# Swapping two groups of work in every fourth iteration: TensorE's first convolution of the next sample ahead of the kernels' products K, ScalarE's rounding of z ahead of K's evictions

## The chip, the cores and the metric

The kernel runs on one core of a Trainium2 chip. The metric is the device time of one execution in microseconds; of the runs of a kernel the median is taken. TensorE (PE) multiplies matrices into PSUM, ScalarE (ACT) and VectorE (DVE) work on tiles element by element, GpSimd (POOL) does small work of that kind, and SyncE (SP) issues the transfers. Each engine executes its own list of instructions strictly in order, and waits on semaphores that the others raise. All times are microseconds.

## The reference

The input x is 64 samples of 64 channels by 1024 points, with one style vector of 128 numbers for each sample. Four blocks follow one another, each `x = x + f(x, style)`. In f there are four layers, each a convolution whose weights are scaled per sample by the style and then normalised:

```python
s = style @ mw.T + mb
weight = SCALE * w * s[:, None, :, None]
demod = lax.rsqrt(jnp.sum(weight * weight, axis=(2, 3)) + EPS)
weight = weight * demod[:, :, None, None]
# 'same':       conv 3 taps + bias
# 'upsample':   transposed conv, stride 2, + bias, then blur (1,3,3,1)
# 'same':       conv 3 taps + bias
# 'downsample': blur (1,3,3,1), then conv, stride 2, + bias
```

The reference computes in float32.

## The kernel before

**Layout.** A sample is held as 128 x 513: the odd points of its 64 channels on partitions 0 to 63, the even ones on 64 to 127. There is no step between layers 1, 2 and 3 that is not linear, so the kernel composes them: for each sample it builds one short filter out of the weights of layers 1 to 3 and the blurs, and applies it to z, the output of layer 0. Near the two ends of a sample the composed filter is not exact, and small separate work ("edges") corrects a few columns.

**Precision.** Products are made in float32r, whose operands are rounded. Each operand is therefore split in two: ScalarE writes the rounded value (`...h`) and VectorE the rest (`...l`), and TensorE makes three products, h by h, h by l and l by h.

**Iterations.** The index n runs over 256 steps, 64 samples in each of the four blocks (in groups of 8 samples the blocks are done as a whole, so block k is n = 64k to 64k+63). For sample n:
- `xhi(n)` (ScalarE, line 733) and `xlo(n)` (VectorE, line 1036) scale and split x. Both are made three samples ahead.
- `conv0(n)` (TensorE): layer 0, 6 matmuls of 512 columns, the first four from xhi, the last two from xlo, into a PSUM bank, of which there are two (n mod 2).
- `zhi(n)` (ScalarE, line 747) and `zlo(n)` (VectorE, line 1042) split z and free that bank.
- `convg(n)` (TensorE): the composed filter, 12 matmuls of 512 columns: 8 with the filter's rounded part gh and 4 with its rest gl.
- `xnew(n)` (VectorE, line 1051): adds the result to x in SBUF; SyncE stores it. In the last block ScalarE has added a bias before that, `xb(n)` (line 755), and xnew waits for it.

**Quads.** The composed filters are built for four samples at a time (q counts these quads). `v_products(q)` (V, 9 matmuls of 256 columns) combines layers 3 and 2; ScalarE and VectorE scale and split the result (`vfull`, `vhi`, `vlo`); `k_products(q)` (K, 15 matmuls of 256 columns) brings in layer 1. V and K use the same two PSUM banks. ScalarE evicts K in two parts of four instructions, `kev(q, 0)` and `kev(q, 1)` (line 787). VectorE applies the blurs to it (`fir_even`, `fir_odd`, lines 1084 to 1096). Then `ghi(q)` (ScalarE, lines 804 and 809) rounds the filter, in two halves, `glo(q)` (VectorE, line 1119) makes the rests, two halves, each waiting for its rounding, and SyncE copies all four to the other half of the partitions. `w3hi` (ScalarE) and `w3s`, `w3lo` (GpSimd, lines 1371, 1377, 1378) prepare the operand of V.

**What sets the order.** Nothing but the code: each engine has a loop over n that calls these functions in a written order. `g_at(n)` gives the quad whose K is made in iteration n: q = n/4 + 1 for n = 4, 8, ..., 248, that is always a quad's first iteration, and the filter is needed from iteration n+4 on. `v_at(n)` places V in iterations n = 4m+1. The first quad's work is spread over a prologue, with exceptions (`V_LATE`, `G_LATE`, `FIRST_GHI = 3`): the filters of quad 1 (samples 4 to 7) are rounded by ScalarE in iteration 3.

TensorE's order in iteration n = 4m is: K(m+1), conv0(n+1), any set-up or edge products, convg(n). ScalarE's order is: w3hi, xhi(n+3), kev part 0, (in iteration 3: ghi(1)), zhi(n+1), kev part 1, ghi, vfull, vhi, xb(n). VectorE's loop (not touched by the change) is: vlo, xlo(n+3), xnew(n-1), in iteration 4m+1 fir_even, then zlo(n+1), fir_odd with xlo behind it, glo. VectorE's prologue ends with xlo(4), vlo(2), glo(1), xlo(5), xnew(2), zlo(4), xlo(6).

Waits that matter here: zhi(n) waits for conv0(n) and for convg(n-2); conv0(n) waits for xhi(n), for zlo(n-2), and ahead of its last two matmuls for xlo(n); convg(n) waits for zlo(n), for xnew(n-2) and for the copies of its filter; V(q) waits for kev(q-1).

Of the kernel before, what the change touches and what calls it, by code (L numbers as in the profile page):

```python
# [27 lines left out]
NN = NS * GS  # L28
NQ = NN // QS
V_LEAD, G_LEAD = 7, 4  # L30
V_LATE, G_LATE = {2: 1}, {1: 0}
# [59 lines left out]
def build(nc, x, ends, pack, taps, w3in, small, sets, out):  # L91
    ctx = ExitStack()
    with ctx:
# [129 lines left out]
        def v_at(n):  # L223
            if n in V_LATE or n in V_LATE.values():
                return (V_LATE[n] + V_LEAD) // QS if n in V_LATE else None
            q, i = divmod(n + V_LEAD, QS)
            return q if i == 0 and 0 <= q < NQ else None

        def g_at(n):
            if n in G_LATE or n in G_LATE.values():  # L230
                return (G_LATE[n] + G_LEAD) // QS if n in G_LATE else None
            q, i = divmod(n + G_LEAD, QS)
            return q if i == 0 and 0 <= q < NQ else None
# [45 lines left out]
        def setup_at(n):  # L279
            k, i = n // NB + 1, n % NB  # L280
            if k == NBLK - 1 and i == LAST_BIAS_S:
                return k, (BIAS_S,)
            return (k, (SECOND_SLOTS if k == 1 else SETUP_SLOTS).get(i, ())) if k < NBLK else (None, ())
# [108 lines left out]
        def _(pe):  # L392
# [67 lines left out]
            def add(out_ap, a, b, first=False, last=False):  # L460

                return pe.matmul(out_ap, a, b, start=first, stop=last, skip_group_check=True)  # L462

            def conv0(n):

                conv0_high(n)
                conv0_low(n)

            def conv0_high(n):
                k, o = where(n)[1], ps[:, ZP + n % 2, :]  # L470
                ah, al, h = w0h[:, k % NW], w0l[:, k % NW], xh[n % 3]
                pe.wait_ge(s["xhi"], n + 1)
                if n >= 2:
                    pe.wait_ge(s["zlo"], n - 1)
                for d in range(2):
                    add(o, ah[:, 2 * d:2 * d + 2, :], h[:, d:d + M], first=(d == 0))
                if n % NB == 0:
                    pe.wait_ge(s["w0l"], k + 1)
                for d in range(2):
                    add(o, al[:, 2 * d:2 * d + 2, :], h[:, d:d + M])  # L480

            def conv0_low(n):
                k, o = where(n)[1], ps[:, ZP + n % 2, :]
                ah, l = w0h[:, k % NW], xl[n % 3]
                pe.wait_ge(s["xlo"], n + 1)
                for d in range(2):
                    m = add(o, ah[:, 2 * d:2 * d + 2, :], l[:, d:d + M], last=(d == 1))
                m.then_inc(s["conv0"], 1)
# [67 lines left out]
            def k_products(q):  # L556

                k = STEPS[q * QS // GS][1]
                h, l, d, dl = w1h[:, k % NW], w1l[:, k % NW], w1d[:, k % NW], w1dl[:, k % NW]
                k6, k45, k23, k01 = (ps[:, VG + i // 2, i % 2 * QS * C:(i % 2 + 1) * QS * C] for i in range(4))  # L560
                early, late = slice(0, 2), slice(2, 4)
                pairs = ((k01, early, 0), (k23, late, 0), (k23, early, 1), (k45, late, 1))
                pe.wait_ge(s["w1hi"], k + 1)
                pe.wait_ge(s["vf"], q + 1)
                pe.wait_ge(s["vh"], q + 1)
                for i, (at, w, o) in enumerate(pairs):
                    add(at, h[:, w, :], vh[:, o, :, :], first=i in (0, 3))
                pe.wait_ge(s["w1l"], k + 1)
                for at, w, o in pairs:
                    add(at, l[:, w, :], vh[:, o, :, :])  # L570
                pe.wait_ge(s["vlp"], q + 1)
                for at, w, o in pairs:
                    add(at, h[:, w, :], vl[:, o, :, :])
                pe.wait_ge(s["vl"], q + 1)
                add(k45, d[:, early, :], vh[:, 2, :, :])
                add(k45, dl[:, early, :], vh[:, 2, :, :])
                add(k6, d[:, late, :], vh[:, 2, :, :]).then_inc(s["K"], 1)
# [65 lines left out]
            idle_products(14)  # L643
            pe.wait_ge(s["z0"], 1)
            for n in range(NN):
                if g_at(n) is not None and n not in G_LATE:
                    k_products(g_at(n))
                if n == 0:
                    conv0_low(1)
                    convg(0)  # L650
                    k_products(1)
                elif n + 1 < NN:
                    conv0(n + 1)
                if n in V_LATE:
                    v_products(v_at(n))
                k, stages = setup_at(n)
                for stage in stages:
                    setup(k, stage)
                if n == FIRST_BIAS_U:
                    setup(0, BIAS_U)  # L660
                k, stage = edge_at(n)
                if k is not None and stage < 3:
                    edge(k, stage)
                    for job in behind(k, stage):
                        setup(*job)
                if n > 0:
                    convg(n)
                if k is not None and stage == 3:
                    edge(k, stage)
                    for job in behind(k, stage):  # L670
                        setup(*job)
                if v_at(n) is not None and n not in V_LATE:
                    v_products(v_at(n))
# [3 lines left out]
        def _(act):  # L677
# [45 lines left out]
            def xhi(n):  # L723
                st, k, b, sl = where(n)
                act.wait_ge(s["S0"], k + 1)
                if k == 0:
                    p, use = pair_of(n)
                    act.wait_ge(s_in[p], 16 * use)
                else:
                    act.wait_ge(s["eap"], applied(st))  # L730
                if n >= 3:
                    act.wait_ge(s["conv0"], n - 2)
                act.activation(xh[n % 3][:, 0:XW], X[:, sl, :], ACT.Copy, scale=tab["S0"][:, k, b:b + 1]) \  # L733
                    .then_inc(s["xhi"], 1)

            def zhi(n):
                st, k, b, sl = where(n)
                act.wait_ge(s["conv0"], n + 1)
                if k:
                    act.wait_ge(s["bv2"], k + 1)  # L740
                elif n >= FIRST:
                    act.wait_ge(s["rest"], 1)
                else:
                    act.wait_ge(s["bx0"], 1)
                if n >= 2:
                    act.wait_ge(s["convg"], n - 1)
                act.activation(zh[n % 2][:, ZPAD:ZPAD + M], ps[:, ZP + n % 2, :], IDENT,  # L747
                               bias=tab["bx"][:, k, b:b + 1]).then_inc(s["zhi"], 1)
# [140 lines left out]
            for n in range(2, NN):  # L889
                if v_at(n + 1) is not None and n + 1 not in V_LATE:  # L890
                    w3hi(v_at(n + 1))
                if n + 3 < NN:
                    xhi(n + 3)
                if g_at(n) is not None:
                    kev(g_at(n), 0)
                if n == FIRST_GHI:
                    ghi(g_at(n - 2))
                if n + 1 < NN:
                    zhi(n + 1)
                if n in V_LATE:  # L900
                    vfull(v_at(n))
                    vhi(v_at(n))
                if g_at(n) is not None:
                    kev(g_at(n), 1)
                if g_at(n - 2) is not None and n != FIRST_GHI:
                    ghi(g_at(n - 2))
                if v_at(n - 1) is not None and n - 1 not in V_LATE:
                    vfull(v_at(n - 1))
                    vhi(v_at(n - 1))
                k, stages = setup_at(n - 1)  # L910
                if RECIP in stages:
                    setup(k, RECIP)
                k, stages = setup_at(n)
                for stage in stages:
                    if stage != RECIP:
                        setup(k, stage)
                if n == FIRST_VAR:
                    act.wait_ge(s["Dp"], 1)
                    act.activation(var[:, :, FIRST:], fl[:, 512:512 + LC].rearrange("p (l b) -> p l b", b=NB)[:, :, FIRST:], IDENT,
                                   bias=eps[:, 0:1], scale=SCALE * SCALE).then_inc(s["var0"], 1)  # L920
                if n == FIRST_ROOT:
                    root(slice(0, NLAY), NPART, slice(FIRST, NB))
                if where(n)[1] == NBLK - 1:
                    xb(n)
# [734 lines left out]
```

## Time and profile before

| | us |
|---|---|
| median of 3 runs | 1302.7 |
| lowest and highest | 1302.08, 1303.91 |
| the profiled execution | 1303.89 |
| its span | 1302.0 |
| TensorE busy in the span | 1291.3 (99%) |
| VectorE busy | 1101.5 (85%) |
| ScalarE busy | 922.4 (71%) |
| GpSimd busy | 359.1 (28%) |

The span runs from the first to the last instruction of the program; the execution's time is 1.9 longer. The mean granted clock of TensorE is 0.998 of its full 2.4 GHz. A matmul's record begins when it starts and ends when its results are out; the next matmul starts before that, so the records of back-to-back matmuls overlap, and the distance from start to start is the pace.

### The profile page before, as it was taken

To read this page: it belongs to the slowest core of one execution; us is meant where nothing else is said; L and a number is where in the kernel's file an instruction comes from. 1 tells how busy PE (TensorE), PEld (TensorE's weight loads), DVE (VectorE), ACT (ScalarE), POOL (GpSimd) and SP (SyncE) were. 2 spreads that over 40 slices of the span, in tenths; PEclk is the share of its full clock that TensorE was granted. 3 is DMA by queue.
4 is the path that set the end of the run, shared out by engine and by line. 5 is a ranking of instruction groups with operands and counts; after the bars stand their busy time and mean duration, and the time that the engine had idled before them with its cause. 6 is when DMAs were issued, how large, how long until landed. Compare 5 with 4: busy or idle time off the path is not lost.

```text
span 1302.0 us, 20375 instructions
## 1 busy us (share of the span) xinstructions
PE 1291.3 (99%) x6553; PEld 1076.5 (83%) x6553; DVE 1101.5 (85%) x1795; ACT 922.4 (71%) x1773; POOL 359.1 (28%) x640
## 2 busy tenths in 40 slices
PE   8999999999999999999999999999999999999998
PEld 6888888888888888888888888888888888888887
DVE  7999888998898889878889798988878878888885
ACT  6767576676675766766767667667677787787784
POOL 5142311141313212115222222122422252322311
PEclk9999999999999999999999999999999999999999
DMA  9354465545564455655446554556554276565543
GB/s 327 103 168 119 144 179 165 164 116 164 174 174 144 123 155 166 182 151 168 130 152 177 153 164 121 154 172 174 161 158 128 77 159 188 163 189 156 165 126 96
DMA packets 95369, 203.39 MB, mean 156 GB/s; under 512 B 10720, under 2 KB 12256, under 8 KB 95264
## 3 DMA queue, kind: packets, MB, share of 16 engines
q1 hardware_dynamic: 95040, 201.91, 54.0%
q8 instruction: 54, 0.88, 0.3%
q14 instruction: 51, 0.42, 0.1%
q10 hardware_dynamic: 224, 0.18, 0.0%
HBM read 72.39 MB, written 67.24 MB: 107 GB/s over the span
## 4 chain that ended last, share of the span: by engine, by line
PE 98%; DVE 1%; ACT 0%; issue 0%; POOL 0%; POOLq 0%; DVEq 0%; ACTq 0%
PE ps L462 96%; PE ps L586 1%; PE ps L398 1%; DVE scr L945 0%; ACT gh L815 0%; ACT vf L771 0%; PE ps L420 0%; DVE scr L955 0%; DVE scr L954 0%; DVE xl L1036 0%; DVE w2l L1245 0%; DVE w3q L1163 0%; ACT xh L733 0%; POOL scr L1416 0%; POOL scr L1415 0%
## 5 line engine op out<-in xcount | busy, mean ns | idle before, releaser
L462 PE MATMUL ps<-zh,gh 128*128 128x512 f32 (+1 forms) x1028 | 407.0, 396 | 0.2 <-ACT gh L815 0.2
L462 PE MATMUL ps<-zl,gh 128*128 128x512 f32 (+1 forms) x1028 | 405.5, 394 | 0.0
L747 ACT ACTIVATE zh<-ps,t_bx 128x512 fp32r<-128x512 f32 x256 | 175.3, 685 | 285.4 <-PE ps L462 284.4
L462 PE MATMUL ps<-zh,gl 128*128 128x512 f32 (+1 forms) x1028 | 282.2, 395 | 0.0
L787 ACT ACTIVATE kp<-ps,t_T1s 64x256 f32<-64x256 f32 x508 | 210.6, 463 | 66.3 <-PE ps L462 61.4
L1051 DVE SCALAR_TENSOR_TENSOR X<-ps,t_D,X 128x512 f32<-128x512 f32 x255 | 190.1, 745 | 61.1 <-PE ps L462 34.6
L462 PEld LDWEIGHTS ps<-zh,gh 128*128 128x128 f32 x1028 | 193.9, 189 | 46.9 <-DVE zl L1042 1.3
L462 PEld LDWEIGHTS ps<-zl,gh 128*128 128x128 f32 x1028 | 194.1, 189 | 45.0
L462 PEld LDWEIGHTS ps<-zh,gl 128*128 128x128 f32 x1028 | 194.0, 189 | 45.1
L1042 DVE SCALAR_TENSOR_TENSOR zl<-ps,t_bx,zh 128x512 fp32r<-128x512 f32 x256 | 190.7, 745 | 42.9 <-ACT zh L747 40.2
L1377 POOL TENSOR_TENSOR w3h<-w3q,w3h 64x256 fp32r<-64x256 f32 x63 | 69.1, 1097 | 548.5 <-ACT w3h L761 535.0
L1036 DVE SCALAR_TENSOR_TENSOR xl<-X,t_S,xh 128x513 fp32r<-128x513 f32 x256 | 190.7, 764 | 2.5
L733 ACT ACTIVATE xh<-X,t_S 128x513 fp32r<-128x513 f32 x256 | 183.3, 716 | 1.2
L462 PE MATMUL ps<-xl,w0h 128*128 128x512 f32 x512 | 160.6, 395 | 2.8 <-DVE xl L1036 2.8
L462 PE MATMUL ps<-xh,w0l 128*128 128x512 f32 x512 | 161.1, 396 | 0.0
L462 PE MATMUL ps<-xh,w0h 128*128 128x512 f32 x512 | 161.1, 395 | 0.0
L1084 DVE SCALAR_TENSOR_TENSOR gf<-kp,gf 128x384 f32<-128x384 f32 x256 | 153.2, 598 | 6.7
L1119 DVE TENSOR_TENSOR gl<-gf,gh 64x896 fp32r<-64x896 f32 x126 | 137.9, 1094 | 16.9 <-ACT gh L809 14.4
L809 ACT ACTIVATE gh<-gf 64x896 fp32r<-64x896 f32 x126 | 120.0, 952 | 3.6
L462 PEld LDWEIGHTS ps<-xl,w0h 128*128 128x128 f32 x512 | 96.0, 188 | 26.6 <-issue 2.3
L462 PEld LDWEIGHTS ps<-xh,w0l 128*128 128x128 f32 x512 | 96.4, 188 | 23.3
L462 PEld LDWEIGHTS ps<-xh,w0h 128*128 128x128 f32 x512 | 87.4, 188 | 11.4
(226 smaller groups left out, 1494.5 us busy)
## 6 DMA issues: line engine op xcount, KB each, us to landing
out_x<-X SPq DMA_DIRECT2D x255, 256.5 KB, 5.2
X<-out_x SPq DMA_DIRECT2D x96, 513.0 KB, 7.1
gh<-gh SPq DMA_DIRECT2D x127, 240.0 KB, 3.0
gl<-gl SPq DMA_DIRECT2D x127, 240.0 KB, 3.7
X<-x_in SPq DMA_DIRECT2D x32, 513.0 KB, 7.2
pk<-taps_in SPq DMA_DIRECT2D x3, 512.0 KB, 12.3
pk<-pack_in SPq DMA_DIRECT2D x3, 352.0 KB, 12.5
pk<-sets_in SPq DMA_DIRECT2D x4, 256.0 KB, 8.4
```

The lines of the kernel that those rows point to most:

```text
L398: m = pe.matmul(fl[h * C:(h + 1) * C, at:at + n], a, b, start=first, stop=last, skip_group_check=True)
L462: return pe.matmul(out_ap, a, b, start=first, stop=last, skip_group_check=True)
L733: act.activation(xh[n % 3][:, 0:XW], X[:, sl, :], ACT.Copy, scale=tab["S0"][:, k, b:b + 1]) \
L747: act.activation(zh[n % 2][:, ZPAD:ZPAD + M], ps[:, ZP + n % 2, :], IDENT, bias=tab["bx"][:, k, b:b + 1]).then_inc(s["zhi"], 1)
L787: return act.activation(kp[rows, to, i, :], got[of, :, j, :], ACT.Copy, scale=tab["T1s"][of, k, b:b + 1])
L809: act.activation(dst, gf[rows], ACT.Copy).then_inc(s["gsh"], 1)
L1036: dve.scalar_tensor_tensor(xl[n % 3][:, 0:XW], X[:, sl, :], tab["S0"][:, k, b:b + 1], xh[n % 3][:, 0:XW].bitcast(F32), ALU.mult, ALU.subtr ...
L1042: dve.scalar_tensor_tensor(zl[n % 2][:, ZPAD:ZPAD + M], ps[:, ZP + n % 2, :], tab["bx"][:, k, b:b + 1], zh[n % 2][:, ZPAD:ZPAD + M].bitcas ...
L1051: dve.scalar_tensor_tensor(X[:, sl, 0:M], ps[:, OP + n % 2, :], tab["D3"][:, k, b:b + 1], X[:, sl, 0:M], ALU.mult, ALU.add).then_inc(s["xn ...
L1084: return dve.scalar_tensor_tensor(dve_out, kp[rows, of, i, :], factor, dve_out, ALU.mult, ALU.add)
L1119: dve.tensor_tensor(dst, gf[rows], own(gh, h)[1].bitcast(F32), ALU.subtract).then_inc(s["gsl"], 1)
L1377: link(pool.tensor_tensor(w3h[C:128, 1], w3q[C:128, 1], hi[C:128, 1], ALU.subtract))
```

## The change

In TensorE's loop the two lines that call `k_products` move behind the block that calls `conv0(n + 1)`. In ScalarE's loop the two lines that call `zhi(n + 1)` move ahead of those that call `kev(.., 0)` and, in iteration 3, `ghi`.

```diff
@@ TensorE's loop
             for n in range(NN):
-                if g_at(n) is not None and n not in G_LATE:
-                    k_products(g_at(n))
                 if n == 0:
                     conv0_low(1)
                     convg(0)
                     k_products(1)
                 elif n + 1 < NN:
                     conv0(n + 1)
+                if g_at(n) is not None and n not in G_LATE:
+                    k_products(g_at(n))
                 if n in V_LATE:
                     v_products(v_at(n))
@@ ScalarE's loop
                 if n + 3 < NN:
                     xhi(n + 3)
+                if n + 1 < NN:
+                    zhi(n + 1)
                 if g_at(n) is not None:
                     kev(g_at(n), 0)
                 if n == FIRST_GHI:
                     ghi(g_at(n - 2))
-                if n + 1 < NN:
-                    zhi(n + 1)
                 if n in V_LATE:
                     vfull(v_at(n))
```

## Rows read from the trace of the kernel before

**Rows 1.** The page, busy us (share of the span) x instructions of each engine
```profile
PE 1291.3 (99%) x6553; PEld 1076.5 (83%) x6553; DVE 1101.5 (85%) x1795; ACT 922.4 (71%) x1773; POOL 359.1 (28%) x640
```

**Rows 2.** Windows: stretch, its length, busy of each engine, PEclk, DMA share, GB/s
```profile
26.90:30.30 3.40, 3.40 (x10) 2.65 (x9) 3.27 (x7) 3.30 (x5) 1.28 (x1) 0.50 1.04 404
...
100.00:1200.00 1100.00, 1100.00 (x5607) 917.27 (x5606) 938.89 (x1522) 782.27 (x1504) 299.45 (x515) 1.00 0.55 155
```

**Rows 3.** Timeline of TensorE, first products of K: start, us, what, idle before
```profile
606.89 0.63 PE L462 MATMUL ps<-vh,w1h 128*128 128x256 f32 x4
...
626.50 0.63 PE L462 MATMUL ps<-vh,w1h 128*128 128x256 f32 x4
```

**Rows 4.** Timeline of TensorE, iterations 3 and 4
```profile
42.87 0.69 PE L462 MATMUL ps<-xl,w0h 128*128 128x512 f32 x2
...
46.18 0.64 PE L462 MATMUL ps<-vh,w1h 128*128 128x256 f32 x4
...
47.96 0.62 PE L462 MATMUL ps<-xh,w0h 128*128 128x512 f32 x2
...
48.89 0.63 PE L462 MATMUL ps<-xl,w0h 128*128 128x512 f32 x2
49.36 0.39 PE L462 MATMUL ps<-zh,gh 128*128 128x512 f32 x1
```

**Rows 5.** Timeline of ScalarE, an ordinary quad (n = 116): K's evictions
```profile
608.85 1.67 ACT L787 ACTIVATE kp<-ps,t_T1s 64x256 f32<-64x256 f32 x4 [0.69 <-PE ps L462]
...
611.25 1.67 ACT L787 ACTIVATE kp<-ps,t_T1s 64x256 f32<-64x256 f32 x4
```

**Rows 6.** Timeline of VectorE, the same quad: the first instruction of fir_even
```profile
613.73 0.73 DVE L1088 TENSOR_TENSOR kp<-kp 128x128 f32<-128x128 f32 x1
```

**Rows 7.** Timeline of VectorE, last block: xnew(192), zlo(195), zlo(239)
```profile
992.45 0.75 DVE L1051 SCALAR_TENSOR_TENSOR X<-ps,t_D,X 128x512 f32<-128x512 f32 x1 [1.77 <-ACT X L755]
...
1001.46 0.74 DVE L1042 SCALAR_TENSOR_TENSOR zl<-ps,t_bx,zh 128x512 fp32r<-128x512 f32 x1
...
1219.60 0.74 DVE L1042 SCALAR_TENSOR_TENSOR zl<-ps,t_bx,zh 128x512 fp32r<-128x512 f32 x1
```

**Rows 8.** Timeline of TensorE, last block: first products of convg(195), convg(239)
```profile
1002.38 0.39 PE L462 MATMUL ps<-zh,gh 128*128 128x512 f32 x1
...
1221.53 0.40 PE L462 MATMUL ps<-zh,gh 128*128 128x512 f32 x1
```

**Rows 9.** Timeline of ScalarE, iteration 3: ghi(1), zhi(4)
```profile
42.18 0.40 ACT L804 ACTIVATE gf<-kp 128x256 f32<-128x256 f32 x1
42.61 1.93 ACT L809 ACTIVATE gh<-gf 64x896 fp32r<-64x896 f32 x2
44.57 0.69 ACT L747 ACTIVATE zh<-ps,t_bx 128x512 fp32r<-128x512 f32 x1
```

**Rows 10.** Timeline of VectorE, end of its prologue: glo(1), xlo(5), zlo(4)
```profile
44.44 2.20 DVE L1119 TENSOR_TENSOR gl<-gf,gh 64x896 fp32r<-64x896 f32 x2
46.67 1.12 DVE L1036 SCALAR_TENSOR_TENSOR xl<-X,t_S,xh 128x513 fp32r<-128x513 f32 x1
...
48.37 0.74 DVE L1042 SCALAR_TENSOR_TENSOR zl<-ps,t_bx,zh 128x512 fp32r<-128x512 f32 x1
```

**Rows 11.** DMA issues: x count, KB each, median us to landing
```profile
gl<-gl SPq DMA_DIRECT2D x127, 240.0 KB, 3.7
```

**Rows 12.** Timeline of GpSimd, w3lo(3)
```profile
45.85 1.39 POOL L1377 TENSOR_TENSOR w3h<-w3q,w3h 64x256 fp32r<-64x256 f32 x1 [12.46 <-ACT w3h L761]
```

**Rows 13.** Timeline of TensorE, its two longest waits, and the pace after
```profile
18.38 0.73 PE L462 MATMUL ps<-xl,w0h 128*128 128x512 f32 x2 [0.67 <-DVE xl L1036]
...
25.36 0.70 PE L462 MATMUL ps<-xl,w0h 128*128 128x512 f32 x2 [2.09 <-DVE xl L1036]
...
27.20 0.63 PE L462 MATMUL ps<-zl,gh 128*128 128x512 f32 x1
27.62 0.63 PE L462 MATMUL ps<-zh,gh 128*128 128x512 f32 x1
```

## Prediction

> **What bounds the kernel now.** I read the page's busy times first, then the windows, then the timelines of single engines. TensorE is busy 99% of the span, VectorE 85%, ScalarE 71% [rows 1]. The windows say where the missing 1% lies: from 100 to 1200 us TensorE is busy for all 1100 us, at granted clock 1.00 [rows 2]; its idle time is at the two ends. A busy matmul record is longer than the distance to the next one, so short pauses could hide in it. The pace rules them out: K of one quad starts at 606.89, of the next at 626.50 [rows 3], 19.61 us, and of the 63 such distances more than 40 are 19.59 to 19.62; the longer ones hold set-up or edge products or lie at the start. So a quad is a fixed string of matmuls that never waits, and an order of the same matmuls cannot shorten it. What the change can do is add a wait, where a result that was just in time is asked for earlier or comes later. TensorE's lost time is never given back, since it has no later idle time to use up.
>
> **The change in an ordinary quad (n = 4m, from n = 8).** No instruction is added or removed and no DMA is touched; one group swaps places on each of two engines. Call the quad's start T (there K starts now). K lasts 1.78 us (46.18 to 47.96) and the convolution conv0 1.40 (47.96 to 49.36) [rows 4].
> TensorE: conv0(n+1) starts at T instead of T+1.78, K ends 1.40 later, convg(n) starts at T+3.18 either way. conv0(n+1) needs xhi, xlo of n+1 and zlo(n-1); the last is already waited for by convg(n-1), and VectorE makes xlo(n+1) back in iteration n-2, so that two whole iterations (1.40 of conv0 and 12 products of 0.235, 4.2 us each) lie between; 1.78 less of that does no harm. Cost 0.
> ScalarE: now the four evictions of kev part 0 run from T+1.96 (608.85) to 610.52, z fills the time to 611.25, and part 1 runs to 612.92, T+6.03 [rows 5]. After: z runs while TensorE is in K, at about T+1.5; the eight evictions start at K's end, 1.40 later, and run in one piece. The z between them (0.71 with its issue) is gone, so kev ends 1.40 - 0.71 = 0.69 later, T+6.72 or 613.61. What is queued behind it: xb in the last block, xhi(n+4), zhi(n+2); and VectorE's fir_even waits for kev. In blocks 0 to 2 fir_even starts at 613.73 now, behind xnew(n), which waits for convg(n) [rows 6]. 613.61 is still ahead of it: cost 0, by a margin of 0.12. If that cover were gone too, VectorE would be a little later, and it has 1 us or more in most quads before zlo(n+3) is asked for. V, the next user of the same PSUM banks, comes behind conv0(n+2) and two convg, at T + 3.18 + 2.82 + 1.40 + 2.82 = T+10.2, and kev's end at T+6.72 is far ahead. Cost 0.
>
> **The last block (n from 192).** Here xb(n) follows kev on ScalarE and VectorE's xnew(n) waits for xb (992.45, idle 1.77 before it, ended by xb [rows 7]). So there the 0.69 goes into VectorE's queue whole, up to zlo(n+3). For n = 192 that zlo ends at 1001.46 + 0.74 = 1002.20, and convg(195) starts at 1002.38 [rows 7, 8]: 0.18 to spare. 0.69 - 0.18 = 0.51, and 0.05 for the semaphore: a stall of **0.56 us**. The 14 other such pairs have 0.97 to 2.53 to spare; the usual one is 1219.60 + 0.74 against 1221.53, 1.19 [rows 7, 8]. None stalls. Bounds: 0 (something ahead of xnew gives the time back) to 0.69.
>
> **The start (n = 3 and 4).** This is the only place where a wait has no slack. In iteration 3 ScalarE makes ghi(1) and then z(4): 42.18, 42.61, 44.57 [rows 9]. After, z(4) stands ahead and must wait for conv0(4), whose last products are at 42.87 + 0.69 = 43.56 [rows 4]. z(4) then runs from 43.60 and ghi(1) from 43.60 + 0.59 = 44.19, 2.01 later than 42.18; its two roundings start at 44.62 and 45.60. VectorE's glo(1) (2.20 us for two) now starts at 44.44, when VectorE comes to it [rows 10]. It will have to wait for the first rounding: 45.61, which is 1.17 later. Behind it on VectorE stands xlo(5), at 46.67 now, for 1.12 us; after: 47.84 to 48.96.
> And conv0(5) is asked for 1.78 us earlier: it starts at 46.18, its first four products take 0.93, and its last two want xlo(5) at 47.11. They start at 48.96 + 0.09 = 49.05. Stall: 49.05 - 47.11 = **1.94 us**. Before, they started at 48.89 with xlo(5) ready at 47.79, so 1.10 of slack hid everything. K(2) and convg(4) follow, the latter at 51.3 instead of 49.36. zlo(4) (48.37 + 0.74 now [rows 10]) comes at 50.3, and gl(1), issued about 47.9 with 3.7 to landing [rows 11], at 51.6; its products are due at 53.2. No second wait.
> Bounds: xlo took 1.12 there and not 0.74 as zlo does. VectorE and GpSimd overlap at that place: GpSimd's w3lo runs 45.85 to 47.24 [rows 12]. With 0.74 in its place the stall is 1.56. Since w3lo waits for a rounding that stands behind ghi(1) on ScalarE, it moves along and I take 1.94. From above, a third rounding-long wait (0.95) gives 2.9; from below, 0 if the records hide a slack that I don't see.
> The Trainium skill (SBUF — State Buffer, "Who interferes with whom") says that a VectorE instruction with two SBUF inputs and a GpSimd instruction that reads SBUF exclude one another for their whole length. By it xlo(5), with X and xh from SBUF, is held as it is now; the 0.38 more in its row agrees.
>
> **Sum.** 1.94 + 0.56 = 2.5 us. The profiled execution took 1303.89 (span 1302.0 and 1.9 around it); after: 1306.4. The median of the runs is 1302.7, the profiled one at the upper end of 1302.08 to 1303.91, so against the median: **1305.2**. That is +0.19%, and I call no change what is within 0.2% (2.6 us), about what a measurement of this kernel can tell. The forecast lies just inside.
>
> **Rivals.**
> A, slower: the stall takes the clock down. TensorE's clock fell once inside the run: it idled 2.09 us before 25.36 [rows 13], and from 26.9 to 30.3 the clock was 0.50 [rows 2], its lower level of 1.2 GHz. Before 18.38 it idled 0.67 and the clock stayed up [rows 13]. My stall, about 1.8 of idle time, lies between, nearer to the 2.09. The price from the same place: 3.4 us of products at a distance of 0.42 to 0.43 (27.20 to 27.62 [rows 13]) are 8, and at the pace of 2.4 GHz (two in 0.47, 48.89 to 49.36 [rows 4]) each would take 0.234: 8 x 0.193 = 1.55 us. The place is n = 4; it decides from an idle time somewhere between 0.67 and 2.09. Time: 1302.7 + 4.0 = 1306.7. Against it: before 25.36 TensorE had also small products and another 0.24 of idle time behind it, here it is dense on both sides.
> The Trainium skill (TensorE: Matmul & The Clock Gate, "What's actually happening") ties the low level to a stretch in which TensorE was idle throughout. By that rule this stall would not be enough and the sum stays at 2.5; the trace's drop, behind a stall with work on both sides, speaks against reading it so strictly.
> B, no loss: xlo(5) comes in time, because glo(1) doesn't wait or because DMA-bound work at the start shifts. Then only the 0.56 of the last block is left, or 0: 1302.7 to 1303.3. For it: all of the 1.94 hangs on one instruction order. Against it: that order is fixed in the code, and each row of it is in the trace.
> C, faster: z made earlier removes waits of convg(n+1) for zlo(n+1). At two of 62 quads that zlo ends 0.05 us before it is used, elsewhere 0.3 or more, so TensorE's pauses for it total under 0.2 us. With neither stall: 1302.5; more only if the matmul pace itself (0.235 us per 512 columns) gets better, for which no row speaks.
> D, a stall in every quad of the last block: if VectorE lost the 0.69 and did not make it up by the next quad. 15 x (0.69 + what piles up) would be some 5 us, 1308. Against it: behind zlo(n+3) VectorE again waits for ScalarE's vhi, which is late by only some 0.3.
>
> **How the numbers follow.** Forecast 0.52, A 0.26, B 0.14, C 0.04, D 0.04. The forecast's own range is 1303.8 to 1306.3; its upper quarter (0.15) is over +2.6. Slower by over 0.2%: A, D and that quarter, 0.45. Faster by over 0.2%: 0.03. Within: 0.52. Range: 1302.6, which takes in most of B, to 1307.4, which takes in A with 0.7 for the spread of the runs.
>
> **What would show it.** In the trace after: TensorE idle about 1.8 us once, at 47.3, released by VectorE's xl line; the xl before it starts near 47.8, and ghi near 44.2. The granted clock around 50 us decides A. K to K stays 19.61 in ordinary quads. In the quad of n = 192 K to K is 0.5 longer. ScalarE's eight evictions in one piece of 3.35 us, ending 0.69 later within the quad. TensorE's work without waits (its start at 26.3 and its end at 1298) must be the same but for the two stalls. The prediction is wrong if xlo(5) is not what TensorE waits for at n = 4, if any ordinary quad is longer, or if the time is under 1302.5 or over 1307.5.

## The result and the profile after

The changed kernel takes 1306.43 us (median of 8 runs, 1305.16 to 1307.92), the kernel before in the same comparison 1303.88 (8 runs, 1302.08 to 1305.38). The ratio is 1.0026, 95% interval 1.0017 to 1.0034: slower by 2.2 to 4.4 us. The medians lie 2.55 apart; forecast was +2.5. As a time, 1305.2 was forecast within 1302.6 to 1307.4; the 1.2 us more come from the kernel before, whose median was 1302.7 when the forecast was made and 1303.88 in this comparison.

The page: the span is 3.8 us longer (1305.8 against 1302.0) and TensorE executes the same number of matmuls. It waited for xl (line 1036) three times where the kernel before waited twice, 2.8 us in all.

```profile
span 1305.8 us, 20375 instructions
...
PE 1292.1 (99%) x6553; PEld 1077.3 (83%) x6553; DVE 1092.8 (84%) x1795; ACT 922.5 (71%) x1773; POOL 361.0 (28%) x640
```

The waits of TensorE in the kernel after (us in total, times, longest):

```profile
PE ps L462 <- DVE xl L1036: 5.3, 3, 2.1
PE ps L462 <- ACT w3h L849: 2.2, 1, 2.2
PE ps L441 <- DVE zl L1029: 1.2, 1, 1.2
```

Iterations 3 and 4 on TensorE, which answer to [rows 4]: conv0(5) now starts at 46.88, and its last two products stand at 49.66.

```profile
43.51 0.70 PE L462 MATMUL ps<-xl,w0h 128*128 128x512 f32 x2
44.05 0.40 PE L462 MATMUL ps<-zh,gh 128*128 128x512 f32 x1
...
46.88 0.63 PE L462 MATMUL ps<-xh,w0h 128*128 128x512 f32 x2
47.34 0.63 PE L462 MATMUL ps<-xh,w0l 128*128 128x512 f32 x2
49.66 0.74 PE L462 MATMUL ps<-xl,w0h 128*128 128x512 f32 x2 [1.68 <-DVE xl L1036]
50.23 0.64 PE L462 MATMUL ps<-vh,w1h 128*128 128x256 f32 x4
...
52.00 0.39 PE L462 MATMUL ps<-zh,gh 128*128 128x512 f32 x1
```

ScalarE there (for [rows 9]) makes z(4) first, idle 1.33 before it:

```profile
44.25 0.69 ACT L747 ACTIVATE zh<-ps,t_bx 128x512 fp32r<-128x512 f32 x1 [1.33 <-PE ps L462]
44.84 0.41 ACT L804 ACTIVATE gf<-kp 128x256 f32<-128x256 f32 x1
45.27 1.93 ACT L809 ACTIVATE gh<-gf 64x896 fp32r<-64x896 f32 x2
```

And VectorE (for [rows 10]) waits 1.22 for the rounding, with xlo(5), xnew(2) and zlo(4) queued behind:

```profile
46.26 2.21 DVE L1119 TENSOR_TENSOR gl<-gf,gh 64x896 fp32r<-64x896 f32 x2 [1.22 <-ACT gh L809]
48.49 1.10 DVE L1036 SCALAR_TENSOR_TENSOR xl<-X,t_S,xh 128x513 fp32r<-128x513 f32 x1
49.52 0.74 DVE L1051 SCALAR_TENSOR_TENSOR X<-ps,t_D,X 128x512 f32<-128x512 f32 x1
50.18 0.74 DVE L1042 SCALAR_TENSOR_TENSOR zl<-ps,t_bx,zh 128x512 fp32r<-128x512 f32 x1
```

Everything here is 0.66 later than in the profile before for reasons ahead of the change (convg(3) starts at 44.05 instead of 43.39). With that taken off, ghi(1), glo(1) and xlo(5) are where the prediction put them. From the second pair of products (47.34) to the third (49.66) there are 2.32 us, 1.84 more than two products take. The granted clock stays at 1.00 behind it (the last number but two of each row):

```profile
30.30:50.00 19.70, 18.02 (x89) 14.66 (x88) 16.14 (x25) 14.79 (x28) 5.83 (x5) 1.00 0.40 115
50.00:60.00 10.00, 10.00 (x56) 8.61 (x55) 9.72 (x16) 6.30 (x13) 2.88 (x4) 1.00 0.38 117
```

An ordinary quad, ScalarE (for [rows 5]) and VectorE (for [rows 6]). The quad starts at 609.80; z is made while K runs, the eight evictions stand in one piece and end at 616.53, that is 6.73 behind its start (6.03 before). fir_even starts 6.85 behind, as before (6.84):

```profile
611.39 0.69 ACT L747 ACTIVATE zh<-ps,t_bx 128x512 fp32r<-128x512 f32 x1 [0.34 <-PE ps L462]
613.17 3.36 ACT L787 ACTIVATE kp<-ps,t_T1s 64x256 f32<-64x256 f32 x8 [1.09 <-PE ps L462]
```
```profile
615.98 0.75 DVE L1051 SCALAR_TENSOR_TENSOR X<-ps,t_D,X 128x512 f32<-128x512 f32 x1 [1.55 <-PE ps L462]
616.65 0.70 DVE L1088 TENSOR_TENSOR kp<-kp 128x128 f32<-128x128 f32 x1
```

To place the rest, each profiled span is cut at the starts of convg(3), (4), (191) and (254) on TensorE. These are differences of start times in the traces, one profile each. The last column says whether the granted clock fell to 0.50 near 27 us:

| kernel | to convg(3) | 3 to 4 | 4 to 191 | 191 to 254 | rest | span | clock fell near 27 |
|---|---|---|---|---|---|---|---|
| before | 43.39 | 5.97 | 933.41 | 309.11 | 10.14 | 1302.02 | yes |
| after | 44.05 | 7.95 | 933.90 | 309.61 | 10.27 | 1305.77 | yes |
| ghi first | 42.97 | 6.78 | 933.90 | 309.48 | 9.68 | 1302.80 | yes |
| not first | 41.42 | 5.96 | 933.87 | 309.49 | 9.81 | 1300.55 | no |
| middle | 41.89 | 5.96 | 933.86 | 309.13 | 9.79 | 1300.63 | no |
| xlo(5) first | 41.86 | 6.31 | 934.27 | 311.03 | 10.56 | 1304.03 | no |
| TensorE only | 42.87 | 6.77 | 934.26 | 312.40 | 9.27 | 1305.56 | yes |
| ScalarE only | 43.44 | 6.94 | 933.56 | 312.42 | 9.45 | 1305.81 | yes |
| more idle products | 42.11 | 6.00 | 933.41 | 310.56 | 9.98 | 1302.07 | no |
| the same, again | 42.21 | 5.95 | 933.40 | 309.21 | 9.34 | 1300.10 | no |

So the 3.75 us are: 0.66 and 0.13 at the two ends, which move from run to run; 1.98 at n = 4; 0.49 spread over the middle; 0.50 in the last block. Of that 0.50, about 0.19 stand at n = 194 and 195, 0.17 at n = 211 and 212, and the rest is spread out. The wait of the last block is this one: zlo(195) on VectorE, and convg(195) right behind it.

```profile
1004.79 0.74 DVE L1042 SCALAR_TENSOR_TENSOR zl<-ps,t_bx,zh 128x512 fp32r<-128x512 f32 x1
```
```profile
1005.58 0.50 PE L462 MATMUL ps<-zh,gh 128*128 128x512 f32 x1
```

### The profile page after: what moved, and what is told of

The parts are those of the page before. It is cut to its first block, busy times and chain, and to the rows that moved or that the text cites. A ratio compares the mean times of both kernels' runs of the same rounds, so it can differ in the third digit from the quotient of the medians.

```text
span 1305.8 us, 20375 instructions
## 1 busy us (share of the span) xinstructions
PE 1292.1 (99%) x6553; PEld 1077.3 (83%) x6553; DVE 1092.8 (84%) x1795; ACT 922.5 (71%) x1773; POOL 361.0 (28%) x640
## 4 chain that ended last, share of the span: by engine, by line
PE 97%; DVE 1%; issue 0%; ACT 0%; DMA 0%; POOL 0%; DVEq 0%; POOLq 0%; ACTq 0%
PE ps L462 96%; PE ps L586 1%; PE ps L398 1%; DMA pk<-taps_in 0%; DVE xl L1036 0%; DVE gf L1084 0%; DVE kp L1217 0%; DVE scr L945 0%; PE ps L420 0%; DVE scr L955 0%; DVE scr L954 0%; ACT gh L809 0%; DVE t_T1s L1201 0%; DVE gf L1090 0%; DVE scr L956 0%
## 5 line engine op out<-in xcount | busy, mean ns | idle before, releaser
L1084 DVE SCALAR_TENSOR_TENSOR gf<-kp,gf 128x384 f32<-128x384 f32 x256 | 152.8, 597 | 6.7
L462 PEld LDWEIGHTS ps<-xh,w0h 128*128 128x128 f32 x512 | 91.5, 188 | 17.1
```

What stands on the lines that cost most here:

```text
L1084: return dve.scalar_tensor_tensor(dve_out, kp[rows, of, i, :], factor, dve_out, ALU.mult, ALU.add)
```

## The experiments

**ghi first.** The changed kernel with ScalarE's old order in iteration 3 alone.

```diff
+                if n == FIRST_GHI:
+                    ghi(g_at(n - 2))
                 if n + 1 < NN:
                     zhi(n + 1)
                 if g_at(n) is not None:
                     kev(g_at(n), 0)
-                if n == FIRST_GHI:
-                    ghi(g_at(n - 2))
```

> The changed kernel, but in iteration 3 ScalarE makes ghi(1) ahead of zhi(4), as before the change. My theory (the loss at the start is ghi(1) -> glo(1) -> xlo(5) -> last two products of conv0(5)): ghi(1) starts some 2 us earlier than in the changed kernel, xlo(5) ends about 1.17 us earlier, TensorE's stall in conv0(5) shrinks from 1.84 to about 0.75 us and does not vanish, since conv0(5) is still asked for 1.78 us earlier. Time 1.1 us under the changed kernel, about 2 over the one before. Rival (the stall comes from the earlier conv0(5) alone): stall stays 1.8. Rival (the order on ScalarE alone): stall 0.

Ratio to before 1.0012 (1.0003 to 1.0021). Its stall is the smaller one:

```profile
47.40 0.74 PE L462 MATMUL ps<-xl,w0h 128*128 128x512 f32 x2 [0.51 <-DVE xl L1036]
```

From convg(3) to convg(4) it takes 6.78, 0.81 over before where the changed kernel takes 1.98 over. Both rivals fall: with TensorE's swap in place, ScalarE's swap in iteration 3 is worth 1.17, and 0.81 is left for TensorE's in iteration 4.

**not first.** Both swaps, from n = 8 on.

```diff
+                late = n > QS
-                if g_at(n) is not None and n not in G_LATE:
+                if g_at(n) is not None and n not in G_LATE and not late:
                     k_products(g_at(n))
...
+                if g_at(n) is not None and n not in G_LATE and late:
+                    k_products(g_at(n))
```

ScalarE's loop has the same condition.

> Both swaps, but only from n = 8 on: iterations 3 and 4 are as before the change. My theory: no stall at n = 4, K to K of the first quads as before, time about 1.9 us under the changed kernel and about 1.1 over the kernel before; what is left is 0.16 at n = 195, up to 0.2 at n = 212, and some 0.013 us in each of 60 quads (0.8 us). Rival (what was lost at the start is the spread of the start-up, not the change): time as the changed kernel, 2.5 to 3.4 over the kernel before.

Ratio 1.0003 (0.9994 to 1.0012). 3 to 4 takes 5.96: the stall is gone, and the median is 0.55 over before. What remains in the middle and the last block (933.87, 309.49) is 0.84 over before, against the 1.1 expected; the main difference is at n = 211 and 212, where up to 0.2 was expected and this profile lost 0.03.

**xlo(5) first.** The changed kernel; in VectorE's prologue the two lines `glo(1)`, `xlo(5)` change places.

> The changed kernel with one more swap: in VectorE's prologue xlo(5) stands ahead of glo(1). My theory (the stall in conv0(5) is nothing but xlo(5) queued behind glo(1), which waits for the late ghi(1)): xlo(5) runs right behind vlo(2), about 3.5 us earlier, conv0(5) never waits, and the stall of 1.84 us is gone although ghi(1) is as late as in the changed kernel. zlo(4) and the copies of gl(1) have over 0.5 us to spare. K to K of the second quad falls from 18.88 to 16.9 us, time 1.8 to 2.0 us under the changed kernel, about 1.1 over the one before. Rival (ghi(1) itself, or something else behind it, is waited for next): convg(4) stalls instead, by 1 us or more.

Ratio 1.0010 (1.0001 to 1.0018). xlo(5) runs right behind vlo(2), and conv0(5) waits no more:

```profile
42.89 0.76 DVE L1036 SCALAR_TENSOR_TENSOR xl<-X,t_S,xh 128x513 fp32r<-128x513 f32 x1
44.07 2.20 DVE L1119 TENSOR_TENSOR gl<-gf,gh 64x896 fp32r<-64x896 f32 x2 [0.43 <-ACT gh L809]
```
```profile
45.59 0.64 PE L462 MATMUL ps<-xl,w0h 128*128 128x512 f32 x2
46.07 0.64 PE L462 MATMUL ps<-vh,w1h 128*128 128x256 f32 x4
...
48.17 0.47 PE L462 MATMUL ps<-zh,gh 128*128 128x512 f32 x1 [0.16 <-issue]
...
50.28 0.49 PE L462 MATMUL ps<-zh,gl 128*128 128x512 f32 x1
```

That confirms the chain up to xlo(5), and part of the rival with it: convg(4) now loses time twice, 0.34 ahead of its first product and 0.35 inside, most of it ahead of the products with gl (50.28). zlo(4), which ended at 47.71, is ruled out. The trace has the landings of the copies of quad 1's filter: the second of gh landed at 48.08, 0.09 ahead of the first product, and the second of gl at 50.23, 0.05 ahead of the first product that reads it. So these copies, which start behind the late ghi(1), are what is waited for next; the 0.5 us to spare that I had expected for them was not there. In the changed kernel the stall for xlo(5) hid it (the copies of gh had landed at 50.32, convg(4) started at 52.00). Of the 1.98 this version gets back 1.29. (The last block took 1.4 more than in the changed kernel, at n = 211; a kernel with the old order lost as much there, see below.)

**TensorE only and ScalarE only.** One swap each, the other engine as before.

> TensorE's swap alone, ScalarE as before. My theory: the two swaps belong together. K ends 1.4 us later and kev part 0, z, part 1 follow it, so kev ends 1.4 later and not 0.7: in blocks 0 to 2 fir_even starts 0.6 later (stalls only near n = 51, 115, 179, 0.3 to 0.5 each), in the last block xnew is 1.4 later against slacks of about 1.2, a stall of about 0.2 in most of its quads and about 1.2 at n = 195. At the start the stall in conv0(5) is about 0.75. Sum about 5 us over the kernel before, more than the changed kernel. Rival (ScalarE's swap is what costs, TensorE's is free): within 1 us of the kernel before.

> ScalarE's swap alone, TensorE as before. My theory: all eight evictions now wait for conv0(n+1), which stands behind K, and end about 1.6 us later than before: fir_even 0.9 later in blocks 0 to 2, xnew 1.6 later in the last block, where a quad then stalls 0.4 (10 to 13 quads), 1.4 at n = 195, 0.5 to 0.7 at n = 51, 115, 179. At the start only 0.16, since conv0(5) still stands behind K(2). Sum 6 to 8 us over the kernel before. The quads of blocks 0 and 1 keep 19.61 us and not 19.62, if that small difference comes from TensorE's order. Rival (TensorE's swap is what costs): within 1 us of the kernel before.

TensorE only: 1.0037 (1.0024 to 1.0051), 4.8 us, as expected. ScalarE only: 1.0022 (1.0013 to 1.0031), 2.9 us, where I had expected 6 to 8; its profiled execution was at the upper end of its runs. Both rivals fall, each swap costs by itself. In the last block each takes 3.3 us more than before in its profile. But 0.5 and 1.4 of that stand at n = 211 and 212, a place where a kernel with the old order lost 1.4 too (see below); from n = 213 on the stalls add up to 2.6 with TensorE's swap alone and 1.8 with ScalarE's. With the whole change (after, ghi first, not first) the last block takes 0.4 to 0.5 more.

The quads from n = 216 to 240 take 19.59 to 19.61 from K to K in the kernel before. With TensorE's swap alone six of them take 19.86 to 20.01, with ScalarE's alone all seven take 19.75 to 19.85. That is 0.25 to 0.4 and 0.15 to 0.25 more, where 0.2 and 0.4 were expected: kev ends 1.4 and 1.3 later within these quads (7.45 and 7.30 behind the start, 6.03 before), not 1.4 and 1.6.

At the start TensorE's swap alone costs 0.80, as expected. ScalarE's alone costs 0.97, not 0.16: what I had left out is zlo(4), two places behind xlo(5) on VectorE. It ended at 50.32, and convg(4) started at 50.38 instead of 49.42:

```profile
49.59 0.73 DVE L1042 SCALAR_TENSOR_TENSOR zl<-ps,t_bx,zh 128x512 fp32r<-128x512 f32 x1
```

And ScalarE only has 933.56 in the middle, TensorE only 934.26: the slower middle goes with TensorE's order.

At n = 195 I had expected 1.2 and 1.4 and got 0.1 in both. VectorE between xnew(192) and zlo(195), in the kernel with TensorE's swap alone:

```profile
994.99 0.75 DVE L1051 SCALAR_TENSOR_TENSOR X<-ps,t_D,X 128x512 f32<-128x512 f32 x1 [1.77 <-ACT X L755]
995.66 0.61 DVE L1088 TENSOR_TENSOR kp<-kp 128x128 f32<-128x128 f32 x1
996.31 0.69 DVE L1090 SCALAR_TENSOR_TENSOR gf<-kp 128x512 f32<-128x512 f32 x1
996.92 0.28 DVE L1092 SCALAR_TENSOR_TENSOR gf<-kp 128x128 f32<-128x128 f32 x1
...
998.88 1.92 DVE L1084 SCALAR_TENSOR_TENSOR gf<-kp,gf 128x384 f32<-128x384 f32 x3
...
1002.71 0.74 DVE L1042 SCALAR_TENSOR_TENSOR zl<-ps,t_bx,zh 128x512 fp32r<-128x512 f32 x1
```

xnew to the end of zlo is 8.46 us here and 9.75 in the kernel before [rows 7]. There L1092 took 1.11 instead of 0.28, and the three L1084 2.51 instead of 1.92:

```profile
993.12 0.53 DVE L1088 TENSOR_TENSOR kp<-kp 128x128 f32<-128x128 f32 x1
...
994.30 1.11 DVE L1092 SCALAR_TENSOR_TENSOR gf<-kp 128x128 f32<-128x128 f32 x1
...
997.04 2.51 DVE L1084 SCALAR_TENSOR_TENSOR gf<-kp,gf 128x384 f32<-128x384 f32 x3
```

GpSimd does edge work in that stretch. Its line 1496 runs beside VectorE's line 1092 in the kernel before. With TensorE's swap alone it has ended at 996.13, 0.8 ahead of that line:

```profile
993.99 1.27 POOL L1496 TENSOR_TENSOR xe<-xe,t_S 128x384 f32<-128x384 f32 x1
```
```profile
995.11 1.02 POOL L1496 TENSOR_TENSOR xe<-xe,t_S 128x384 f32<-128x384 f32 x1
```

In the changed kernel the same GpSimd instruction (997.13 to 998.16) stands beside line 1090, and there it is line 1090 that is long, and line 1092 takes 0.33:

```profile
997.27 1.43 DVE L1090 SCALAR_TENSOR_TENSOR gf<-kp 128x512 f32<-128x512 f32 x1
```

So most of the delay was given back by instructions that met less of GpSimd's work. How much comes back depends on what stands beside what: 1.3 us here, 0.5 in the changed kernel.

**middle.** Both swaps for n = 8 to 188 alone.

> Both swaps for n = 8 to 188 only; the start and the last block are as before the change. My theory: nothing waits anywhere in these quads, so the only thing left is the pace: where K stands behind conv0, a quad takes 0.010 us more. From convg(4) to convg(191): 933.9 us as in the changed kernel (933.4 before); from convg(191) to convg(254), where the order is the old one, about 0.5 less than in a kernel with the swap on the same chip (309.1 to 310.6, by chip). Rival (the small difference is drift between runs): 933.4, or a value between.

One run, 1302.43. 933.86 in the middle, 309.13 in the last block: where the order is the old one, so is the time. Seven profiles of the table agree: 933.40 or 933.41 in the three with the old order throughout, 933.86 to 933.90 in the four with both swaps (before and the two with more idle products; after, ghi first, not first and middle). The other three are at 933.56 (ScalarE's swap alone), 934.26 (TensorE's alone) and 934.27 (xlo(5) first). The last two have single waits in addition: xlo(5) first loses its 0.35 inside convg(4), TensorE's swap alone 0.11, 0.11 and 0.13 at n = 11, 15 and 51. With these taken off they are at 933.92 and 933.91. The two kernels with longer stalls, below, run the first 1.4 and 1.3 us of this stretch at the lower clock; from convg(5) to convg(191) they are 0.44 over before, the others with both swaps 0.46 to 0.51. That this half microsecond goes with TensorE's order is shown; how it comes about is open.

**Longer stalls.** To see where the clock falls, the changed kernel with ghi(1)'s first copy made 3 and 7 times, each waiting for the one before (on a semaphore of its own, `pause`). The edit for three copies:

```diff
+                for i in range(2 if q == 1 else 0):
+                    act.activation(gf[:, 0:NT:NT - 1], kp[:, 1:8:6], ACT.Copy).then_inc(s["pause"], 1)
+                    act.wait_ge(s["pause"], i + 1)
                 act.activation(gf[:, 0:NT:NT - 1], kp[:, 1:8:6], ACT.Copy).then_inc(s["gfe"], 1)
```

> The changed kernel with ghi(1) made later: ScalarE makes the first copy of ghi(1) three times instead of once, each waiting for the one before, 0.45 to 0.5 us each. The stall in conv0(5) grows from 1.84 by 1.0 to about 2.8 us. This asks where a single stall between dense matmuls brings TensorE's clock down. If a stall of over 2.1 us does it, as the one at the start of the kernel before seemed to say, the granted clock is 0.5 for some 3 us behind it and the time is 2.5 us over the changed kernel's; if not, 1.0 over.

> The same with seven copies: the stall in conv0(5) is about 4.7 us. I expect the granted clock to be 0.5 for some 3 us behind it, the time 2.9 + 1.5 us over the changed kernel's. If the clock stays up even here, the fall near 27 us has another cause than a stall (the share of work before it).

One run each, 1310.38 and 1311.34 us. TensorE idled 2.61 and 4.36, and both times the granted clock fell to 0.50 once: with three copies from 51.2 to 54.6, after TensorE had gone on at 49.92, with seven from 49.2 to 56.0, while it still idled.

```profile
49.92 0.74 PE L462 MATMUL ps<-xl,w0h 128*128 128x512 f32 x2 [2.61 <-DVE xl L1039]
```
```profile
30.80:51.10 20.30, 17.69 (x91) 14.51 (x90) 15.57 (x24) 14.53 (x29) 5.22 (x5) 1.00 0.45 119
51.30:54.50 3.20, 3.20 (x14) 2.91 (x14) 3.20 (x4) 1.19 (x4) 1.99 (x2) 0.50 0.40 105
```

and with seven copies:

```profile
50.49 0.80 PE L462 MATMUL ps<-xl,w0h 128*128 128x512 f32 x1 [4.36 <-DVE xl L1039]
```
```profile
49.30:55.90 6.60, 5.41 (x20) 5.03 (x21) 6.41 (x8) 1.63 (x5) 4.34 (x5) 0.50 0.58 156
```

**More idle products.** The kernel before, with `idle_products(14)` ahead of the loop made `idle_products(30)`.

> The kernel before with 30 instead of 14 of its idle products ahead of the loop (matmuls whose results nobody reads, 0.118 us each): they fill TensorE's wait from 23.1 to 25.4 us. One profile of a kernel with the same start had no fall of the clock there and began iteration 3 some 1.5 to 2 us earlier than the others. If the wait is what brings the clock down, the granted clock stays at 1.00 from 17 us on, and the time is 1.0 to 1.5 us under the kernel before, whose runs mostly have the fall. Rival (the fall comes from elsewhere, or these products delay conv0(1)): same as before, or slower by up to 0.3.

> The kernel before with 30 idle products once more, on another chip or at another time: the first comparison gave a ratio of 0.9994 with an interval from 0.9985 to 1.0003. If filling the wait keeps the clock up, the ratio is again 0.999 to 0.9995 and the granted clock is 1.00 between 17 and 1300 us; if that profile was luck, 1.000.

Ratio 0.9994 (0.9985 to 1.0003), twice. The medians are 1.09 and 1.10 us under before, but the interval holds 1. The clock stayed up in both profiles. TensorE's wait for xl there is 0.17 in both, where it was 2.09:

```profile
21.75 3.76 PE L441 MATMUL ps<-zl 128*128 128x256 f32 x30
25.68 0.71 PE L462 MATMUL ps<-xl,w0h 128*128 128x512 f32 x2 [0.17 <-DVE xl L1036]
```

In the second comparison all 11 runs lie from 1301.64 to 1302.47; those of the kernel before lie around 1302.1 (5 of 15, 1301.74 to 1302.41, each with a mean granted clock of 1.0) and around 1303.5 (10, 1302.99 to 1303.88, each with 0.998 or 0.999). The first comparison is less clear: 9 of 11 runs lie from 1302.73 to 1303.85 and two at 1305.7, where the kernel before has 1302.97 to 1305.63. This version is faster than the changed kernel by more than the intervals; against the one before it is probably 1 us faster, and not proved so.

## Why the prediction was right

The direction and the main place held; +2.5 was forecast, the ratio says +3.4, its interval 2.2 to 4.4. So the time landed at the border of my own "within 0.2%", by the ratio on its far side. That it came this near is in part luck, as the terms show: the stall at the start, 1.94 of the 2.5, was right; the 0.56 of the last block was not, and terms that the sum lacked made up for it. As a time, 1306.43 is nearer to rival A's 1306.7 than to 1305.2, since the kernel before was slower in this comparison; it is the trace, with the clock at 1.00 behind the stall, that tells the two apart.

- **The start.** Forecast 1.94, measured 1.84 at the products and 1.98 from convg(3) to convg(4), since the matmuls right behind a wait start 0.1 later. Each link was seen: z(4) 1.33 idle, ghi(1) 2.0 late, glo(1) waiting 1.22, xlo(5) 1.10 long beside GpSimd's w3lo. Undoing one link took away its part: ghi first 1.17 of the 1.98, xlo(5) first the whole wait for xlo(5), of which 0.69 came back as waits for the copies of the filter. The prediction let those copies through with "no second wait". In the changed kernel that held, but only because the stall in front of them was longer.
- **Ordinary quads.** kev ends 0.70 later (0.69 forecast), fir_even doesn't move. But "cost 0" was wrong by 0.010 us a quad, 0.49 in the middle. The prediction excluded that the order of matmuls that never wait matters, and called itself wrong if any ordinary quad were longer. By that sign it failed on this term: K to K in ordinary quads is 19.59 to 19.64, where it was 19.59 to 19.61. It is the term that was missing.
- **The last block.** xnew is 0.70 late within the quad of n = 192, as forecast, but of the 0.56 stall only some 0.17 to 0.19 came, because VectorE's instructions got shorter where they met less of GpSimd's work: xnew to the end of zlo(195) took 9.24 us instead of 9.75. The prediction had put this down only as its lower bound. There was another wait of 0.17 at n = 212:

```profile
1093.72 0.47 PE L462 MATMUL ps<-zh,gh 128*128 128x512 f32 x1
1094.04 0.39 PE L462 MATMUL ps<-zl,gh 128*128 128x512 f32 x1
```

K's last product starts at 1093.52, so this one is 0.09 late, and the next 0.08 more. zlo(212) had been ready for 0.29. The second of gh's copies landed at 1093.63; in the kernel before it had landed 0.40 ahead of need. The change did not issue it later: it was issued 7.0 us ahead of need in both, and took 6.99 us to land instead of 6.59. Over all twelve profiles this one copy took from 5.8 to 8.4 us, and TensorE waited in just those seven in which it took over 6.9. The kernel with more idle products, with the old order, is one of them: it waited 1.22 there in its first profile (1.4 lost, in the table's 310.56) and not in its second. So this wait is not shown to be the change's; ghi first and not first, with both swaps, didn't have it.

```profile
1090.40 0.47 PE L462 MATMUL ps<-zh,gh 128*128 128x512 f32 x1 [1.22 <-issue]
```

- **The sum** was near because errors partly cancel: 0.4 too much at n = 195; 0.5 too little in the middle, and about 0.3 too little in the rest of the last block, half of it the wait at n = 212. From convg(3) to convg(254) the profiles differ by 2.97, where 2.5 was forecast; the 0.8 at the two ends move from run to run.
- **Rival A** (the clock falls) didn't come in the one profile with 1.68 us of idle time, but did in the one with 2.61: the price was real, 3.4 us at half speed. Whether it comes in some of the unprofiled runs at 1.68 is not known. B, C and D didn't come. D came in part where only one swap was made: in those kernels the quads from about n = 216 to 240 do stall, with kev 1.3 to 1.4 late against slacks of about 1.2.

## What to carry to other kernels

When one engine is busy 99% and nothing waits, a reordering has no gain to make there; look only for waits that it adds. They are found where a consumer is moved forward and its producer back at once, most of all in a prologue, whose slack is small: list for each moved step the slack of everything behind it in every queue, two places behind too (zlo(4) behind xlo(5)). When one wait is removed, look for the next that it had hidden: here the copies of the filter stood behind xlo(5). A swap that makes sense on one engine may need its partner on the other: in the quads from n = 213 on the two together cost 0.1 us, TensorE's alone 2.6 and ScalarE's alone 1.8.

## What the runs showed of the hardware

- **The clock.** A single idle time of TensorE at n = 4, between dense matmuls and at full clock: 0.51 and 1.68 us left it at 2.4 GHz; with 2.61 and 4.36 it was at 1.2 GHz for 3.4 and 6.8 us. That is one profile for each length. At the start, behind the same 2.1 us of idle time, it fell in six profiles and stayed up in four (before, after, ghi first, TensorE only, ScalarE only and three copies; not first, middle, xlo(5) first and seven copies). The program is the same up to there, so it varies from run to run, and one profile at 1.68 and one at 2.61 don't place a border between them. The six that fell had idled 0.50 to 1.54 us ahead of conv0(0)'s last products, some 7 us earlier, and the four that stayed up 0.37 or less; whether that decides it is not shown. The fall is worth about 1.4 us of a run, and by the clocks of the 15 runs above it explains most of the spread of the kernel before. The Trainium skill (TensorE: Matmul & The Clock Gate, "What's actually happening") ties the fall to a stretch in which the engine was idle throughout; a fall behind 2.1 us of idle time with work on both sides, in six profiles here, is more than that tells.
- **The pace.** 512 columns in float32r take 0.233 us back to back at full clock (0.427 at the lower one), and a string of 96 matmuls in which no wait is seen depends on the order of its groups by 0.010 us in 19.6. That is a mean over 47 quads, 0.44 to 0.51 us in all, in each of the seven profiles with both swaps there.
- **Overlap of VectorE and GpSimd.** The same VectorE instruction took 0.28 and 1.11 us (line 1092), the latter beside GpSimd's line 1496, and line 1090 took 0.69 and 1.43 in the same way. So moving VectorE against GpSimd can give a delay back, or add one. The Trainium skill (SBUF — State Buffer, "Who interferes with whom") has a VectorE instruction with two inputs in SBUF and a GpSimd instruction that reads SBUF exclude one another; the rows agree.
